# Attention inside a fused two-layer kernel: value products of two pairs of key tiles in one run, denominators directly behind them, maxima three pairs ahead

## What is computed

```python
q = conv1x1(qn, wq, bq); k = conv1x1(vn, wk, bk); v = conv1x1(vn, wv, bv)   # after group norms
q, k, v = (to_tokens(q), to_tokens(k), to_tokens(v))       # 16 heads x 4096 tokens x 32
attn = jax.nn.softmax(jnp.einsum('bhnd,bhmd->bhnm', q, k) * scale, axis=-1)
out = jnp.einsum('bhnm,bhmd->bhnd', attn, v)
```

## Time and profile before

| | |
|---|---|
| median of three runs | 6027.35 us |
| span of the profiled execution | 6025.9 us |
| busy over the whole span: PE, DVE, ACT, POOL | 5368.7 (89%), 4431.8 (74%), 2685.4 (45%), 3764.1 (62%) us |
| attention, from the first score to the last read-out | 443.5 to 4022.8 us |
| DVE reductions of maxima, whole kernel | 4096, 681 ns mean |
| POOL additions of the sums (L491) | 1024, 2385 ns mean |
| chain that ended last | lies in the last projection (from 5740 us) and says nothing of the attention |

### The profile page before, as it was taken

One profiled execution on the slowest core, in us unless ns is written; L12 is line 12 of the kernel. 1 busy time (PEld: TensorE's weight loads), 2 busy tenths in 40 slices (PEclk: granted clock), 3 DMA queues, 4 the chain that ended last, 5 costly groups with the idle time before them and its releaser, 6 DMA issues. The chain is left out here.

```text
span 6025.9 us, 84393 instructions
## 1 busy us (share of the span) xinstructions
PE 5368.7 (89%) x24032; PEld 2623.2 (44%) x24032; DVE 4431.8 (74%) x5229; ACT 2685.4 (45%) x4959; POOL 3764.1 (62%) x1636
## 2 busy tenths in 40 slices
PE   7989999999999999999999999963479886889777
PEld 3444444444444444444444444421245453546333
DVE  3248888888888888888888888831269885989833
ACT  1116666666656666666666666640022222222201
POOL 0008888888888888888888888860054652665300
PEclk9979999999999999999999999986789988989889
DMA  3220100100100100100100010013300000000054
GB/s 149 97 88 10 25 12 23 25 12 23 25 12 23 25 12 23 25 12 23 25 17 19 23 25 11 10 36 110 98 5 19 20 19 18 9 24 9 22 181 149
DMA packets 102966, 224.89 MB, mean 37 GB/s; under 512 B 14576, under 2 KB 23792, under 8 KB 99440
## 3 DMA queue, kind: packets, MB, share of 16 engines
q1 hardware_dynamic: 98272, 211.78, 11.5%
q10 hardware_dynamic: 4368, 8.65, 0.4%
HBM read 139.37 MB, written 80.48 MB: 36 GB/s over the span
## 5 line engine op out<-in xcount | busy, mean ns | idle before, releaser
L655 DVE TENSOR_REDUCE b_mx<-b_pmax 128x1 f32<-128x512 f32 x4096 | 2566.5, 681 | 532.5 <-PE b_pmax L511 529.5
L491 POOL TENSOR_TENSOR b_sums<-b_sums,b_prob 128x1024 f32<-128x1024 f32 x1024 | 2442.6, 2385 | 529.9 <-DVE b_sums L680 361.4
L632 ACT ACTIVATE b_prob<-b_pscore 128x512 f32<-128x512 f32 x4096 | 2155.1, 602 | 1328.4 <-PE b_pscore L525 1324.0
L511 PE MATMUL b_pmax<-b_kst,b_qst 96*128 96x512 f32 x4096 | 1773.0, 436 | 53.3 <-DVE b_mx L655 31.3
L525 PE MATMUL b_pscore<-b_qst,b_kst 98*128 98x512 f32 x4096 | 1658.0, 406 | 19.3 <-issue 10.1
L511 PEld LDWEIGHTS b_pmax<-b_kst,b_qst 96*128 96x128 f32 x4096 | 779.9, 190 | 1126.4 <-DVE b_mx L655 984.2
L538 PE MATMUL b_pout<-b_prob,b_vst 128*32 128x512 f32 x8192 | 1094.3, 606 | 0.0
L1249 DVE SCALAR_TENSOR_TENSOR d_dsum<-d_ypad,d_dw,d_dsum 128x3072 f32<-128x3072 f32 x288 | 1018.8, 3537 | 10.1
L525 PEld LDWEIGHTS b_pscore<-b_qst,b_kst 98*128 98x128 f32 x4096 | 778.2, 190 | 394.9 <-issue 229.5
L485 POOL TENSOR_TENSOR b_sums<-b_prob 128x1024 f32<-128x1024 f32 x256 | 612.2, 2391 | 452.6 <-ACT b_prob L632 447.8
L1031 POOL TENSOR_SCALAR d_wtap<-d_bd,d_dw 128x128 f32<-128x128 f32 x288 | 468.5, 1650 | 0.1
(11 more groups left out here) (111 smaller groups left out, 3125.6 us busy)
## 6 DMA issues: line engine op xcount, KB each, us to landing
b_kst<-scratch_kh SPq DMA_DIRECT2D x32, 512.0 KB, 9.2
b_qst<-scratch_qh SPq DMA_DIRECT2D x128, 128.0 KB, 2.5
scratch_att<-b_outn SPq DMA_DIRECT2D x128, 128.0 KB, 2.3
scratch_num<-d_num SPq DMA_DIRECT2D x64, 256.0 KB, 2.0
f_num<-scratch_num SPq DMA_DIRECT2D x8, 2048.0 KB, 10.2
f_rden<-scratch_rden SPq DMA_DIRECT2D x64, 256.0 KB, 9.4
a_x<-in_x SPq DMA_DIRECT2D x4, 2048.0 KB, 14.7
scratch_qh<-a_high SPq DMA_DIRECT2D x8, 1024.0 KB, 4.0
```

Of the source, the lines that this page charges most:

```text
L491: pool.tensor_tensor(acc, acc, p[:, step, :], ALU.add).then_inc(pool_added, 1)
L511: pe.matmul(pmax[max_bank(place_of(u, m))][:], qst[0:SUMS, b, t * P:(t + 1) * P], kst[0:SUMS, par, j * BANK:(j + 1) * BANK], start=True, s ...
L632: act.activation(prob[:, kt % PBUF, half * BANK:(half + 1) * BANK], pscore[score_bank(hs)][:], ACT.Exp, scale=SCALE).then_inc(exped, 1)
L655: dve.tensor_reduce(mx[:, t, j:j + 1], pmax[max_bank(place_of(u, m))][:], AX.X, ALU.max).then_inc(max_read, 1)
```

## The change

`times_v` is no longer issued at every pair but at every second one, two pairs of it in a row and one pair later than before; `denominators` follows it without a product between. All four maxima products of a pair stand among its scores, so PE's order is now S M S M S M S M for two pairs, then `times_v` twice, then, in every second such run, `denominators`. The transpose stands ahead of `times_v`. `EARLY` becomes 3: the maxima run three pairs ahead, so `pack_shift`, the transpose and `copy_shift` move from pair 14 to pair 13, which is an odd one. ACT reads `b_pout` out at tile 4 in place of 1. Number and shape of all operations stay.

```diff
-    EARLY = 2
+    EARLY = 3
@@ turn, on PE
                         for part in range(4):
                             scores(u, 4 * pair + part, par, place % QBUF)
-                            for m in products[part:part + 1] if part < 3 else ():
+                            for m in products[part:part + 1]:
                                 max_product(u + ahead, m, t_par, t_buf)
-                        if pair:
-                            times_v(u, head, par, c, pair - 1)
-                        elif behind:
-                            times_v(u - 1, head, par if c else 1 - par, (c - 1) % UNITS, PAIRS - 1)
-                        for m in products[3:]:
-                            max_product(u + ahead, m, t_par, t_buf)
                         if pair == PAIRS - EARLY and not (final and place == TURN - 1):
                             transpose_shift(u + 1)
+                        if pair % 2 == 0:
+                            continue
+
+
+                        if pair > 1:
+                            times_v(u, head, par, c, pair - 3)
+                            times_v(u, head, par, c, pair - 2)
+                        elif behind:
+                            for p in range(PAIRS - 2, PAIRS):
+                                times_v(u - 1, head, par if c else 1 - par, (c - 1) % UNITS, p)
                         if pair % (OCT // 2) == OCT // 2 - 1:
                             o = pair // (OCT // 2)
                             if o:
@@ after the last turn
-            times_v(ALL - 1, HEADS - 1, 1, UNITS - 1, PAIRS - 1)
+            for p in range(PAIRS - 2, PAIRS):
+                times_v(ALL - 1, HEADS - 1, 1, UNITS - 1, p)
@@ unit, on ACT
-                    if behind and kt == 1:
+                    if behind and kt == 4:
                         read_out(u - 1)
```

## The result

The changed kernel takes 6305.85 us (four runs, 6303.61 to 6309.51) against 6025.44 us before: ratio 1.0462, 95% interval 1.0447 to 1.0477, 280 us slower. The prediction had the sign right and the size wrong: 6071 us, range 6005 to 6110.

The account below looks back on a forecast made before the run. PE, 98% busy, was taken to set the pace, DVE and POOL near behind. Per unit +0.5 - 1.2 + 0.9 + 0.6 - 0.1 = +0.7; 64 units (+42 unrounded) plus 2 gave +44: 6071 us, range 6005 to 6110.

Parts of the forecast that it names:

- Part 1: Two pairs per run: waiting for DVE's banks eats the saved switches, double pair 6.20 us against 6.14, +0.5 a unit.
- Part 2: `denominators` directly behind `times_v` costs 0.88 us in place of 1.17, -1.2 us a unit.
- part 3: Shift at pair 13: block costs +0.9 us a unit, its multiply waiting for POOL another +0.6.
- the additions' growth: DVE's addition grows 0.34 us an octet, from some 1.2 to 2.2 ahead of the shift.
- part 4: The rest: values' copy -0.1 us a unit, ACT's read-out 0, additional maxima +2.4 once, last units 0 to +2.
- the values' copy: Copy behind the reads of pair 1: costs 0.2 to 0.7 us in place of 0.85, -0.1 a unit.
- ends for the block's cost: Limits for the multiply in the shift's block: 1.19 and 2.35 us, where the forecast took 2.1.
- case D: Worse than forecast: `times_v` on `times_v` 1.00, read-out exposed, multiply 2.35; up to +1.2 a unit, 6105 us; chance 0.15.
- A: DVE doesn't hold PE in the runs; POOL then binds at 54.5 us a unit, 5961 us; chance 0.08.
- B: The shift's multiply slips in ahead of POOL's step and takes 0.2 us: 5948 us; chance 0.07.
- C: POOL isn't pushed behind, the shift's multiply stays at 1.2 to 1.5 us: 6015 to 6035 us; chance 0.20.
- E: The forecast itself, all terms as summed: 6045 to 6090 us; chance 0.50.

Follow-up runs that it names:

- experiment 8: The changed kernel with POOL's additions over 64 of 1024 columns and DVE reading half of each maxima bank: 5694.71 us (ratio 0.9454).
- experiment 3: The changed kernel without the second small operation of `pack_shift` and with 7 spare score products on PE: 6037.68 us (ratio 1.0018).
- experiment 2: The changed kernel with 14 spare score products in PE's idle time at the shift: 6201.29 us (ratio 1.0295).
- experiment 6: `pack_shift` as one reduction, remainder left out: changed kernel 5935.52 us; the same with `EARLY` = 2, 5930.68; kernel before, 5956.77.
- experiment 4: The changed kernel with `EARLY` = 2 as before, two-pair runs kept: 5957.91 us (ratio 0.9892).

## Why the prediction was wrong

**Right.** Part 1: 6.18 for 6.20, and experiment 8 shows why. Part 2: 0.87 for 0.88. In part 3, that the multiply waits for POOL, and that the faster octets push it against a step's beginning: 2.26 us median for 2.35 walked, where the sum took 2.1; the additions' growth is 0.35 for 0.34. In part 4, the values' copy: 0.27 us a time in experiment 3 for 0.2 to 0.7. Without the two omissions the change measures 6038 (experiment 3); the sum had +44, the run +12. Some 10 of these 32 us lie in the units between two turns, which the sum did not cost at all; a plain unit is +0.47, less than the sum has without its term for the copy (0.66 + 0.1).

**Wrong: part 3 stops one instruction early.** It walked DVE to the multiply's end and took for the rest the 1.93 us of the earlier trace rows with its 0.17 for the second operation, though that operation reads SBUF twice beside the same POOL. In the kernel before, it fell into the gap of 0.17 that POOL leaves between two steps that depend on one another, 2010.02 (the end of L485 in the earlier trace rows) to 2010.19:

```profile
2010.08 0.17 DVE L666 SCALAR_TENSOR_TENSOR b_mneg<-b_mtop,b_mneg 128x8 f32<-128x8 f32 x1
2010.19 2.35 POOL L491 TENSOR_TENSOR b_sums<-b_sums,b_prob 128x1024 f32<-128x1024 f32 x1 [0.17 <-ACT b_prob L632]
```

(The bracket names ACT; the step waits for ACT's exponentials and for the step before.) At the new place, the step that follows is L485, the first of an octet. It depends on no sum and starts without a gap: in the earlier trace rows 2007.64 comes right upon 2005.30 + 2.38 = 2007.68. The row was there and I had it in hand, but used it only for when a step ends. The missed term is 2.09 us a unit by the rows, 134 us, and at most 164 by experiments 2 and 3. The Trainium skill, SBUF — State Buffer, Who interferes with whom, says of a DVE instruction with two SBUF inputs that it contends with a GpSimd instruction that reads SBUF, and of the holder that the other fully blocks. By that rule the second operation had to be on the list; the runs agree, 2.26 us beside a POOL step of 2.33 and 0.17 with the steps at 0.32.

**Wrong: no term for the clock.** The prediction took 2.4 GHz as given, since the earlier trace rows read 1.00 and PE was 98% busy. With both waits PE idles 3.9 to 4.3 us once a unit, and the granted clock behind it is 0.50 for some 6 us: at least 105 us, by experiment 2. A forecast of a longer wait on PE should have asked what PE's clock does behind it. My ends for the block's cost did not contain it either, so case D ended at 6105.

The trace of the kernel before had the sign. Three of the units between two turns take 59.8 to 60.1 us at a granted clock of 0.97, the two later ones, at 1.00, 57.4. In one of the three, PE waits for the store of the shift, and `times_v` then takes 1.94 us in place of 1.06:

```profile
1792.15 0.49 PE L525 MATMUL b_pscore<-b_qst,b_kst 98*128 98x512 f32 x1 [3.08 <-DMA b_qst<-b_mrow]
...
1794.27 1.94 PE L538 MATMUL b_pout<-b_prob,b_vst 128*32 128x512 f32 x8
```

The mean of the earlier trace rows over 3385 us rounds this away.

The steps from kernel to kernel are 105 us (the idle time filled, experiment 2), 164 (the second operation and 7 spare products less, experiment 3) and 12 (what the prediction had summed). That they make 280 proves nothing, since each is measured against the next. Priced apart from the runs are the 134 of the 164, and the estimate of 13.

**The rivals.** A (DVE doesn't hold PE) fell: the banks do hold it, by experiment 8. The bound by POOL that its sum used, 54.5 us a unit, was right: experiment 6 stands at it. B: the multiply didn't slip in ahead of a step (1.84 to 2.35 us in all units). The same mechanism did decide, but for the second operation, and in experiment 4 in the kernel's favour. C fell with the additions' growth. D and E had the sign, and neither came near the size.

## What to carry to other kernels

A tiny operation that another engine's steps hold up costs what the step in flight has left, whatever its own size (0.17 us alone, up to 2.35 here), and a chain of two such operations can wait twice. Walk the chain to its last instruction against the neighbour's schedule, gaps included, before moving it. Or take a form that didn't wait in any trace: a reduction out of SBUF and an operation that reads PSUM kept their 0.22 and 0.27 us, and experiment 6 is 102 us faster than experiment 3 by that. Where TensorE comes to idle as long as it did here before the clock fell, add the half-clock time behind it as a term of its own, and look in the trace of before for a place where it already fell.

## What the runs showed that I had not expected

- The clock fell to 0.50 behind 3.9 to 4.3 and 3.0 to 3.2 us of idle PE (in all 61 units: those of the two kernels read 0.96 at most), and in 53 of 61 units of the kernel that idles 1.6 to 2.0 us; 14 useless products that left at most 1.2 us idle kept it up in 53 of 61 and made the kernel 105 us faster.
- POOL starts a step that has no semaphore of its own predecessor to await without a gap, and leaves 0.17 us otherwise. That gap was worth 2.1 us a unit to DVE.
- POOL's five steps, its gaps and DVE's addition, which ends 1.08 us behind the POOL step that it meets, take 13.54 to 13.65 us an octet, 54.4 a unit. The three kernels of experiment 6 all stand within 0.5 us of it on average. Behind it lies the next bound: with POOL's steps small a plain unit is still 54.1 us, and only shorter reads of the maxima bring 50.8.
